# Node features of a two-layer graph network: the transposed copy loaded instead of made, and the order tables drawn anew

## What is computed

```python
mask = (adj > 0.0).astype(x.dtype)
xj_proj = x @ W1a
diff = x[:, :, None, :] - x[:, None, :, :]
h = jax.nn.relu(xj_proj[:, :, None, :] + diff @ W1b + b1)
hm = jnp.einsum('bjkh,bjk->bjh', h, mask)
deg = jnp.sum(mask, axis=-1)
return hm @ W2 + deg[..., None] * b2
```

## Time and profile before

| | us |
|---|---|
| median of 3 runs (863.59 to 864.40) | 864.36 |
| the profiled execution | 865.67 |
| its span, first to last instruction | 863.3 |
| PE busy | 786.3 (91%) |
| DVE busy | 747.8 (87%) |
| ACT busy | 638.5 (74%) |
| POOL busy | 512.2 (59%) |

### The profile page before, as it was taken

How to read it: one execution, slowest core, us unless ns; L and a number is a source line. 1 busy time by engine, 2 the same in 40 slices (tenths; PEclk the granted TensorE clock), 3 DMA queues, 4 the chain that set the end, 5 groups by cost and what they waited for, 6 DMA issues and landing times.

```text
span 863.3 us, 26017 instructions
## 1 busy us (share of the span) xinstructions
PE 786.3 (91%) x10368; PEld 653.8 (76%) x10368; DVE 747.8 (87%) x849; ACT 638.5 (74%) x1896; POOL 512.2 (59%) x598
## 2 busy tenths in 40 slices
PE   3779899999999999999999999999999999999963
PEld 2457778778788878788887878888887878887742
DVE  5699998988989899898989989998988989897862
ACT  4636666887878788687878878787877878778551
POOL 5313334775758576675857567584857657365851
PEclk9999999999999999999999999999999999999996
DMA  3432323123232312322232222313231232121000
GB/s 122 114 77 57 93 57 87 32 57 105 49 89 57 106 32 57 100 57 82 57 105 57 70 62 56 99 48 97 56 99 33 57 105 51 51 57 39 2 13 26
DMA packets 31562, 57.54 MB, mean 67 GB/s; under 512 B 8272, under 2 KB 8912, under 8 KB 31440
## 3 DMA queue, kind: packets, MB, share of 16 engines
q1 hardware_dynamic: 31440, 55.86, 25.1%
HBM read 13.90 MB, written 4.19 MB: 21 GB/s over the span
## 4 chain that ended last, share of the span: by engine, by line
PE 58%; issue 16%; ACT 8%; DVE 7%; DMA 6%; SPq 3%; POOL 2%; POOLq 0%; DVEq 0%; ACTq 0%
PE PS L861 13%; PE PS L869 12%; DMA VB<-VN 5%; PE PS L943 3%; PE PS L931 3%; DVE AC L1171 3%; SPq L1830 2%; DVE AC L1192 2%; PE PS L953 2%; ACT AM L1494 2%; PE PS L688 2%; PE PS L847 2%; PE PS L677 2%; PE PS L820 1%; PE PS L950 1%
## 5 line engine op out<-in xcount | busy, mean ns | idle before, releaser
L1192 DVE SCALAR_TENSOR_TENSOR AC<-PS,AC 128x1152 f32<-128x1152 f32 (+2 forms) x279 | 330.5, 1185 | 63.5 <-PE PS L861 62.6
L1171 DVE SCALAR_TENSOR_TENSOR AC<-PS,AC 128x1152 f32<-128x1152 f32 x248 | 288.5, 1163 | 7.5 <-PE PS L869 5.3
L861 PE MATMUL PS<-DM,VA 128*128 128x192 fp8e5 (+1 forms) x1024 | 120.7, 240 | 19.2 <-DMA VB<-VN 7.6
L869 PE MATMUL PS<-DM,VB 128*128 128x192 fp8e5 (+1 forms) x1024 | 120.0, 240 | 10.4 <-DVE AC L1192 9.7
L861 PE MATMUL PS<-DM,VB 128*128 128x192 fp8e5 (+1 forms) x1024 | 119.5, 239 | 0.8 <-DVE AC L1189 0.6
L869 PE MATMUL PS<-DM,VA 128*128 128x192 fp8e5 (+1 forms) x1024 | 119.5, 239 | 0.1
L861 PEld LDWEIGHTS PS<-DM,VA 128*128 128x128 f16 x1024 | 78.3, 98 | 50.8 <-DVE AC L1171 18.3
L1786 POOL TENSOR_TENSOR AC<-AC,SD 128x512 f32<-128x512 f32 (+1 forms) x62 | 63.6, 1048 | 63.2 <-DVE DM L1149 62.0
L869 PEld LDWEIGHTS PS<-DM,VB 128*128 128x128 f16 x1024 | 76.6, 98 | 27.6 <-DVE AC L1192 11.6
L861 PEld LDWEIGHTS PS<-DM,VB 128*128 128x128 f16 x1024 | 83.0, 98 | 1.6 <-DVE AC L1189 1.6
L869 PEld LDWEIGHTS PS<-DM,VA 128*128 128x128 f16 x1024 | 82.9, 98 | 1.0 <-DVE AC L1168 0.6
(11 more groups left out here) (270 smaller groups left out, 2134.9 us busy)
## 6 DMA issues: line engine op xcount, KB each, us to landing
CW<-WM SPq DMA_DIRECT2D x128, 160.0 KB, 2.9
AT<-in_adjt SPq DMA_DIRECT2D x16, 512.0 KB, 3.8
VA<-VN SPq DMA_DIRECT2D x64, 128.0 KB, 2.3
VB<-VN SPq DMA_DIRECT2D x64, 128.0 KB, 2.3
XN<-in_xn SPq DMA_DIRECT2D x16, 256.0 KB, 4.4
out<-YO SPq DMA_DIRECT2D x15, 256.0 KB, 4.0
cs<-in_cst SPq DMA_DIRECT2D x1, 544.5 KB, 3.4
out<-YO SPq DMA_DIRECT2D x2, 128.0 KB, 1.7
```

Of the source, the lines that this page charges most:

```text
L861: last = e.matmul(PS[:, b + i % 2, 256 * (i // 2) + cols.start:256 * (i // 2) + cols.stop], left(lhs, i), d[:, i, :], start=False, stop=Tr ...
L869: last = e.matmul(PS[:, b + 2, 256 * (i // 2) + cols.start:256 * (i // 2) + cols.stop], right(lhs, i), d[:, i, :], start=False, stop=True, ...
L1171: e.scalar_tensor_tensor(dst, tiles(PS[:, b:b + 3, :])[:, :, cols], 0.0, dst, ALU.max, ALU.add).then_inc(s["sx"], 1)
L1192: e.scalar_tensor_tensor(dst, tiles(PS[:, b:b + 3, :])[:, :, cols], 0.0, dst, ALU.max, ALU.add).then_inc(s["sy"], 1)
```

## The change

Four things change.

1. The host passes x a further time, transposed (`xq`, features by graphs by nodes). For each quad SP loads it twice, to partitions 0 to 63 and 64 to 127 of XQ (`load_x`, two DMAs of 64 x 512 float32), as soon as POOL has read the last one (`xql`).
2. ACT rounds the lower copy to float16 into XT0, whose upper half is zero (`x_split` on ACT), and POOL subtracts XT0 from XQ into the node columns of XE (`x_split` on POOL). That gives the high part above and the low part below.
3. `x_turn` on PE multiplies by OV alone, four matmuls for four graphs into one bank, and ACT evicts that bank once, into the overflow columns of XE. `v` waits for POOL's part alone, `seeds` for both.
4. XN has one buffer in place of two: its next load waits for POOL's and ACT's reading of the one before. All tables are written anew.

```diff
-XN = [sb(f"XN{i}", [128, GB, F]) for i in range(2)]
+XN = sb("XN", [128, GB, F])
+XQ = sb("XQ", [128, 4, 128])
+XT0 = sb("XT0", [128, 4, 128], F16)
...
 # the tables, one line each
-("s", "r", "2pe3pb", "", "bpe", "pbt", "", "rpt", "dceee", "t", "eptr", "p", "pd", "p", "", "ebp", "d", "re0", "1"),
+("s", "2pr", "bpb3b", "ep", "p", "tpr", "pe", "t", "dpr", "t", "t", "epee", "edp", "", "e", "pb", "dc", "0", "re1"),
-("sb2bpp", "", "3bdp", "", "dlpt", "pe", "crtp", "t", "t", "ddn", "pn", "bdp", "ed", "d", "ndp", "dd", "p", "r0d1dp", ""),
+("b2s", "3pbp", "d", "", "dt", "tp", "", "lttc", "npn", "pddbb", "pee", "pnd", "pd", "d", "rdp", "", "pd", "dp", "drd01"),
...
 # PE
-            def x_turn(q, k, b, gates):
+            def x_turn(q, b, gates):
...
-                for a in range(2):
-                    o = PS[:, b, 256 * a:256 * a + 256]
-                    x = XHL[g % 2][:, c + a, :, :].rearrange("p k n -> p (k n)")
-                    e.matmul(o[:, nat], x, idb[:], start=True, stop=True)
-                    last = e.matmul(o.rearrange("p (c n) -> p c n", n=64)[:, 0:4:3, :], x, OV[g % 2][:, c + a, :, :],
-                                    start=True, stop=True)
+                for i in range(4):
+                    last = e.matmul(PS[:, b, 128 * i:128 * i + 128], XHL[g % 2][:, c + i, :, :].rearrange("p k n -> p (k n)"),
+                                    OV[g % 2][:, c + i, :, :].rearrange("p k n -> p (k n)"), start=True, stop=True)
...
 # ACT
+            def x_split(q):
+                ac.wait_ge(s["dx"], 32 * (q + 1))
+                ac.wait_ge(s["xql"], q)
+                ac.wait_ge(s["ms"], 1)
+                e.activation(XT0[64:128], XQ[64:128], ACT.Copy).then_inc(s["xqh"], 1)
...
 # POOL
+            def x_split(q):
+                po.wait_ge(s["xqh"], q + 1)
+                po.wait_ge(s["o0"], q - 3)
+                e.tensor_tensor(XE[q % 4][:, :, nat], XQ[:], XT0[:], ALU.subtract).then_inc(s["xql"], 1)
...
 # SP
+            def load_x(q):
+                for h in range(2):
+                    e.dma_start(XQ[64 * h:64 * h + 64], xq[:, 4 * q:4 * q + 4, :]).then_inc(s["dx"], 16)
+
+            def x_split(q):
+                if q + 1 < NQ:
+                    sy.wait_ge(s["xql"], q + 1)
+                    load_x(q + 1)
```

More of the change, by code:

```diff
@@ L455, in turns @@
             def turns(q):
-                for k in range(2):
-                    yield from bank.spare()
-                    here = bank.take()
-                    do("x_turn", q, k, *here)
-                    bank.give(here[0], "xe", 2 * q + k + 1)
-                    yield
+                yield from bank.spare()
+                here = bank.take()
+                do("x_turn", q, *here)
+                bank.give(here[0], "xe", q + 1)
+                yield
             def prep(q):
+                do("x_split", q)
+                yield
                 yield from bank.spare()
@@ L1791, in dgen @@
                     po.wait_ge(s["dd"], RD * t + m + 1)
[L1793 removed]
+            follow(main_order, {"setup": setup, "parts": parts, "count": count, "x_split": x_split, "split_x": split_x, "mask": mask, "split_xg": split_xg, "split_ms": split_ms, "split_x1": split_x1, "split_h": split_h, "s_ov": s_ov, "clear": clear, "scale_u": scale_u, "add_u": add_u, "dgen": dgen, **gpsimd_layer1(e, po, s)})
         def gpsimd_dense(e):
@@ L1922 @@
         "xn": x.transpose(1, 0, 2),
+        "xq": x.transpose(2, 0, 1),
         "w1": w1,
```

47 lines of the change are left out of this document (24 added, 23 removed), and 2 rows, old and new, of the table MAIN.

## The result

| | before | changed |
|---|---|---|
| median (us) | 864.31 | 873.93 (872.22 to 874.78) |
| ratio, with its 95% interval | | 1.0111 (1.0093 to 1.0128) |
| profiled execution | 865.67 | 874.78 |
| its span | 863.3 | 873.1 |

The changed kernel is 9.6 us slower. I had forecast 858.0 and a range of 851 to 868; the sign was wrong and the time lies outside the range.

What follows compares the result with a forecast made beforehand. Bound: DVE's work, about 44.9 us per two steps, plus 4.3 us of waits. Waits falling from 4.30 to 3.89 give 0.41 a pair, 6.2 us over 15 pairs: 864.36 less 6.2, stated as 858.0; range 851 to 868.

Steps and rivals of the forecast that it cites:

- layout by hand: DVE's waits at odd-turn b1, b2, odd-step b3, a3, even-turn b1: 0, 0.78, 0.83, 0.75, 1.3 us.
- The new waits at b3 and a3: Odd step: moving `words`, `out0_a` and `rank_t` opens DVE waits of 0.83 us at b3 and 0.75 at a3.
- b2's: Odd turn: with `rank_ov` gone and `ov` in, DVE's wait ahead of b2 falls from 1.46 to 0.78 us.
- my 3.89: Sum of DVE's waits in a pair of steps: 4.30 us before, 3.89 after, so 0.41 gained.
- my 7: PE: dropping x_turn's 128 identity matmuls saves 7 us of PE time over the kernel.
- 1.16: POOL: the new 128 x 512 subtraction priced at 1.16 us, from the nearest row of the same size.
- the bounds I had set for SP: SP's two new issues a quad could cost 0 to another 7.6 us of PE's waits on VB; taken as 0.
- So the time of two steps is DVE's work, about 44.9 us, and 4.3 us of waits: Whole step pair, 49.2 us: the change leaves DVE's work alone and can win only from the 4.3 us.
- Rival 1: Even turn: POOL's `gd` holds up DVE's `dgen`, 0.3 to 0.5 us a pair behind b1; 863.5 us, chance 0.14.
- The other queues: POOL, SP and start: the subtraction raises POOL from 59% to 63 to 64%, covered on average; SP's cost taken as 0.
- Rival 2: POOL delivers `h` about 3.1 us later, so ACT's `split_h` is late and PE stalls; 869 us, chance 0.15.
- I put 0 for both: Start and end of the execution: no change in time, with 1 us either way.

Runs made afterwards that it cites:

- words_clear: Changed kernel with POOL waiting for `words` on DVE and `h` placed behind it in the even step; 871.32 us, ratio 1.0083.
- h_first: Changed kernel with `h` of the even step ahead of x_split, `add_u` and `scale_u` on POOL; 876.48 us, ratio 1.0141.
- three_edits: words_clear, plus `scale2` on ACT moved behind b2 of the odd step, plus second-layer weight DMAs issued in two halves; 873.06 us, ratio 1.0112.
- no_pool_split: Changed kernel without POOL's subtraction; ACT writes float16 x into both halves of XE (128 x 512); 870.71 us, ratio 1.0068.

## Why the prediction was wrong

**What held.** Each wait of the layout by hand came within 0.3 us, and none came out above it: 0, 0.54, 0.76, 0.64 and 1.03 for 0, 0.78, 0.83, 0.75 and 1.3. The new waits at b3 and a3 are there. Part of the agreement is luck, because passes that were held up fill some of these waits: with `words` and the `dgen` behind b9 free again (`words_clear`), b2's is 1.19 for my 0.78, and all waits of a pair are 4.22 for my 3.89. x_turn's matmuls are gone and PE is 3.5 to 6.4 us less busy for my 7. x_split on POOL takes 1.20 in the mean for 1.16. PE's waits on VB grew by 3.8 us, inside the bounds I had set for SP; 2.9 of it is one wait in the start.

**The step that failed** is the sentence "So the time of two steps is DVE's work, about 44.9 us, and 4.3 us of waits", with the conclusion that the change adds nothing to the first term. It kept the count of DVE's instructions and took their durations for constants. They aren't: `dgen` and `words` depend on what POOL does when they are due. In the most frequent pair the `words` of the even step is 0.74 us longer than before (1.96 for 1.22), the `dgen` behind b9 0.80, and those of the even turn 0.44, 2.0 in all. DVE's work is 46.85 where it was 44.95, and its waits are 3.30 where they were 4.32, which makes 50.15 for 49.27. I had 44.9 and 3.89. The waits fell by more than twice what I forecast; the 1.9 of longer passes is the term that I had put at nothing. The rows for it were there before the result: `dgen` beside POOL, and the mean of `words`, 0.917 where a free one took 0.82. Rival 1 calls the one such meeting in the trace, and that was a misreading: in the kernel before, `words` takes 1.12 to 1.22 in eight of the even steps.

**Rival 1 had the mechanism and the wrong place and size.** I looked for the meeting of `gd` with the even turn's `dgen`, since that guard had visibly been moved. That one came, 0.31 inside the wait ahead of b1, and 0.13 behind b1. I didn't ask the same for every 16-bit pass: `words` has no guard at all, and the guard of a `dgen` holds only what stands behind it in POOL's order, so a POOL that is late with `scale_u` from ahead of it runs into it. In "The other queues" I wrote of POOL's 63 to 64% "On average this is covered"; the 1.2 us more in each step make it later at just the places where it has to be done. The Trainium skill, "SBUF — State Buffer", under "Who interferes with whom", states more than I took from it: a VectorE instruction with two inputs in SBUF meets GpSimd's reads as well, one with a single SBUF input outside the two-port modes doesn't meet it at all; it counts tensor_scalar among the operations that can enter those modes. The trace agrees in all three cases: `words` reads c7 and AM from SBUF (1.97 for 0.82), `dgen` is a 16-bit tensor_scalar (1.35 for 0.55), and the rounds, with one input in PSUM, stay at 1.35 beside POOL.

**Rival 2** (h too late, 869 or more) had the right sign and not the right link: `h_first` gained nothing, and PE waits for GTl once, 1.2 us. The chain that does run through POOL is `scale_u`, then ACT's NNB and SD, then a1.

**"I put 0 for both"**, start and end, with 1 either way, was off by 7.7 us up to the fifth `off` and by 2.8 the other way at the end. What the runs show of it: the first 94 us vary by 3.7 us between kernels with the same start (92.8 to 96.5), and without the loads they take 2.6 less, which is within that. Early in them lies the 2.92 us of wait for V's copy, and the falls of the clock behind it. Between 94 and 194 us two pairs cost 3.6: in the first PE waits 1.22 for V's copy, in the second `words`, the `dgen` behind b9 and those of the even turn are held up as in the regular pairs. Without POOL's subtraction these two pairs cost 2.0 and the first 94 us still 4.7. Which of the changes makes the start longer stays open, and so does what shortens the end.

**What a removed stall is worth.** I expected 8 to 14 us from `words_clear` and 8 to 12 from `three_edits`, and got 2.6 and 0.9. Each edit uncovered the next link: DVE's hold-up, then ACT's SD, behind it POOL's `scale_u`, and at the even turn V's copy. The runs show these links one at a time. In the eleven regular pairs the loss is POOL's subtraction, by `no_pool_split`. How it divides between the held-up passes and POOL's own lateness isn't settled; the one pair with a free `words` and nothing else moved puts that pass alone at 0.98. A full split of the 9.6 us into causes the runs don't give, because the parts don't add.
